# Inverse transform in front of P times V on TensorE, with ScalarE's two copies in that order

## What is computed

```python
# layer 0: window attention whose queries and keys are multiplied in the Fourier domain
qkv3 = ...                      # 1x1 convolution of the group-normalised x, 8x8 windows, 6 heads of 32
o = jnp.fft.irfft2(jnp.fft.rfft2(qp) * jnp.fft.rfft2(kp), s=(8, 8))    # per head and channel
attn = jnp.einsum('bhnd,bhmd->bhnm', o, vv) + bias[None]
attn = jax.nn.softmax(attn, axis=-1)
y = jnp.einsum('bhnm,bhmd->bhnd', attn, vv)
x = x + einsum('bchw,oc->bohw', y, proj_w) + proj_b
# layer 1: a Laplacian and a 1x1 convolution, of the group-normalised x
x = x + conv1x1(xn + laplacian(xn), merge_w) + merge_b
```

## Time and profile before

| | us |
|---|---|
| median of 3 runs | 6069.41 (6067.23 to 6069.91) |
| the profiled execution | 6063.48 |
| its span, first to last instruction | 6061.7 |
| TensorE busy (PE) | 5826.5 |
| VectorE busy (DVE) | 5059.8 |
| ScalarE busy (ACT) | 3165.5 |
| GpSimd busy (POOL) | 2011.1 |

### The profile page before, as it was taken

One profiled execution on the slowest core, in us unless ns is written; L12 is line 12 of the kernel. 1 busy time (PEld: TensorE's weight loads), 2 busy tenths in 40 slices (PEclk: granted clock), 3 DMA queues, 4 the chain that ended last, 5 costly groups with the idle time before them and its releaser, 6 DMA issues.

```text
span 6061.7 us, 210224 instructions
## 1 busy us (share of the span) xinstructions
PE 5826.5 (96%) x93708; PEld 5135.1 (85%) x93708; DVE 5059.8 (83%) x8287; ACT 3165.5 (52%) x6020; POOL 2011.1 (33%) x1286
## 2 busy tenths in 40 slices
PE   7999999999999999999999999999999999999987
PEld 5888888888888888888888888888888888888876
DVE  4777788888888888888888888888888888888876
ACT  2555555555555555555555555555555555555531
POOL 1333333333333333333333333333333333333310
PEclk9999999999999999999999999999999999999999
DMA  4221123323333233332333323332333322222235
GB/s 130 71 58 58 54 75 104 98 81 93 95 104 101 75 92 99 101 97 80 95 101 100 93 80 93 106 101 86 86 96 98 106 84 69 82 79 75 80 93 163
DMA packets 392599, 550.79 MB, mean 91 GB/s; under 512 B 24918, under 2 KB 284825, under 8 KB 391706
## 3 DMA queue, kind: packets, MB, share of 16 engines
q1 hardware_dynamic: 391708, 537.35, 30.9%
HBM read 335.93 MB, written 201.33 MB: 89 GB/s over the span
## 4 chain that ended last, share of the span: by engine, by line
PE 82%; DVE 8%; ACT 7%; issue 1%; DMA 1%; SPq 0%; DVEq 0%
PE b_q L481 22%; PE b_t L570 10%; PE b_s L587 7%; PE b_q L556 7%; PE b_t L546 6%; PE b_s L489 5%; PE b_s L486 5%; PE b_t L528 4%; PE b_s L432 3%; PE b_s L434 3%; PE b_t L518 3%; ACT qkh L940 2%; DVE qkl L874 2%; PE b_s L441 2%; PE b_s L443 2%; PE b_s L442 2%
## 5 line engine op out<-in xcount | busy, mean ns | idle before, releaser
L1047 POOL TENSOR_TENSOR probs<-probs,srec 128x768 f32<-128x768 f32 x512 | 880.7, 1720 | 2211.8 <-DVE srec L923 2211.8
L1036 POOL TENSOR_TENSOR probs<-probs,smax 128x768 f32<-128x768 f32 x512 | 754.1, 1473 | 1519.7 <-DVE smax L885 1519.7
L880 DVE TENSOR_TENSOR probs<-b_s,posb 128x768 f32<-128x768 f32 x512 | 488.3, 954 | 660.3 <-PE b_s L587 659.4
L940 ACT ACTIVATE vs<-b_q 128x192 f32<-128x192 f32 x1024 | 339.2, 331 | 1294.3 <-PE b_q L481 1294.3
L481 PE MATMUL b_q<-wnh,xh 128*128 128x288 f32 x2048 | 700.7, 342 | 67.0 <-DVE qkl L874 65.7
L874 DVE TENSOR_TENSOR qkl<-b_q,qkh 128x384 fp32r<-128x384 f32 x1024 | 566.5, 553 | 176.9 <-ACT qkh L940 139.7
L489 PEld LDWEIGHTS b_s<-yT,wp 128*128 128x128 f32 x4096 | 618.5, 191 | 52.3
L489 PE MATMUL b_s<-yT,wp 128*128 128x128 f32 x4096 | 622.4, 275 | 0.0
L486 PE MATMUL b_s<-yT,wp 128*128 128x256 f32 x2048 | 613.5, 381 | 1.5 <-DVE probs L880 0.9
L481 PE MATMUL b_q<-wnl,xhl 128*128 128x288 f32 x2048 | 606.5, 296 | 0.0
L481 PE MATMUL b_q<-wnh,xhb 128*128 128x288 f32 x2048 | 606.3, 296 | 0.0
(11 more groups left out here) (155 smaller groups left out, 13688.6 us busy)
## 6 DMA issues: line engine op xcount, KB each, us to landing
ld<-in_x SPq DMA_DIRECT2D x192, 512.0 KB, 4.6
late<-x_dram SPq DMA_DIRECT2D x112, 640.0 KB, 4.8
xs<-in_x SPq DMA_DIRECT2D x128, 512.0 KB, 5.4
x_dram<-late SPq DMA_DIRECT2D x128, 512.0 KB, 3.0
out<-late SPq DMA_DIRECT2D x128, 512.0 KB, 3.0
late<-x_dram SPq DMA_DIRECT2D x240, 192.0 KB, 5.4
xs<-in_x SPq DMA_DIRECT2D x128, 256.0 KB, 5.9
x_dram<-late SPq DMA_DIRECT2D x128, 256.0 KB, 3.7
```

The lines of the kernel that those rows point to most:

```text
L880: V.tensor_tensor(scored(i).rearrange("p (t q) m -> p t q m", q=4), scores.rearrange("p (t q m) -> p t q m", q=4, m=N), posb[:, :, :].unsq ...
L940: return A.activation(o, i, ACT.Copy)
L1036: P.tensor_tensor(probs[:, i % 2, :, :], probs[:, i % 2, :, :], smax[:, i % 2, :].unsqueeze(2).broadcast_to([128, 12, N]), ALU.subtract).t ...
L1047: P.tensor_tensor(probs[:, i % 2, :, :], probs[:, i % 2, :, :], srec[:, i % 2, :].unsqueeze(2).broadcast_to([128, 12, N]), ALU.mult).then_ ...
```

## The change

In TensorE's program o moves ahead of y; in ScalarE's program the copy of o (`osb`) moves ahead of the copy of y (`yT`). Nothing else differs, and no wait is added or dropped. After the change the matmuls of o stand on L542 and those of y on L556.

```diff
                 m_slot(2 * j + 1, pair)
+                if pair(1):
+                    pe.wait_ge(prod_done, pair(1)[1])
+                    if pair(0):
+                        pe.wait_ge(lo_out, 2 * j + 2)
+                    for k in range(6):
+                        for g in range(2):
+                            last = mm(o_out_ps[g * N:(g + 1) * N, k * N:(k + 1) * N],
...
+                    last.then_inc(o_mm, 1)
                 if pair(3):
                     k, n = pair(3)
                     pe.wait_ge(pT_out, n)
...
                     last.then_inc(y_mm, 1)
-                if pair(1):
...
-                    last.then_inc(o_mm, 1)
                 if pair(0):
                     pe.wait_ge(lo_out, 2 * j + 2)
...
+                if pair(1):
+                    act.wait_ge(o_mm, pair(1)[1])
+                    copy(osb[:, :, :].rearrange("p k n -> p (k n)"), o_out_ps).then_inc(o_out, 1)
                 if pair(3):
                     act.wait_ge(y_mm, pair(3)[1])
                     copy(yT[:, :, :, :].rearrange("p i w n -> p w i n"),
                          q_banks[:, 2:4, 0:3 * N].rearrange("p w (i n) -> p w i n", n=N)).then_inc(yT_out, 1)
-                if pair(1):
-                    act.wait_ge(o_mm, pair(1)[1])
-                    copy(osb[:, :, :].rearrange("p k n -> p (k n)"), o_out_ps).then_inc(o_out, 1)
```

More of the change, by code:

```diff
@@ L535, in _ @@
                 m_slot(2 * j + 1, pair)
+                if pair(1):
[5 more added lines that the diff above has]
+                            last = mm(o_out_ps[g * N:(g + 1) * N, k * N:(k + 1) * N],
+                                      prod[:, g * 6 + k, :, :].rearrange("p h d -> p (h d)"), inv[:, :],
+                                      start=True, stop=True)
+                    last.then_inc(o_mm, 1)
                 if pair(3):
```

## The result

| | before | after |
|---|---|---|
| median of 4 runs, us | 6068.32 (6065.76 to 6069.91) | 6115.02 (6109.53 to 6121.13) |
| the profiled execution | 6063.48 | 6117.48 |
| its span | 6061.7 | 6115.6 |

The change makes the kernel slower: the ratio is 1.0077, interval 1.0065 to 1.0089, which is 46.7 us (39 to 54). Forecast were +40 and 6109.4. The two profiled executions lie 54.0 us apart, 7 more than the medians, so a sum over their turns comes out some 7 us too large for the median.

A forecast was written before the change was run, and what follows sets the result against it. The prediction took TensorE, 82% of the chain, as the bound; 43.0 us for turns 76 to 511, plus 2 for earlier turns, less 4.8 at changes of image, gave +40, so 6109.4 us, range 6080 to 6132.

The forecast's parts named there:

- Part 1: In TensorE's stretch of o and y: exchanging their matmuls costs 0, bounded at 0.01 us a turn.
- Part 2: At t's second half: it waits for yT, 0.05 us late plus 0.08 for unhidden loads, 0.13 us a turn.
- Rival 1: At t's second half: loads are pulled ahead of the wait, only 0.05 is lost; +11 us, 6080; chance 0.10.
- Part 3, kind 2: Turns 76 to 511 with j mod 4 = 2: each pays 0.13 us; 28.3 us together with j mod 4 = 0.
- Part 3, kind 3: Turns with j mod 4 = 3: 14.2 us; o's wait for qkl replaces y's for probsT within 0.01.
- Part 3, kind 0: Turns 76 to 511 with j mod 4 = 0: each pays 0.13 us; 28.3 us together with j mod 4 = 2.
- Part 3, kind 1: Turns with j mod 4 = 1: VectorE holds s, so 103 of 109 cost 0; 0.8 us for the other six.
- The changes of image, -4.8: Around changes of image: VectorE is the bound for 37 turns' worth, TensorE's delay costs nothing there; -4.8 us.
- Turns before 76: Turns 3 to 75: o's 0.12 earlier start nearly pays back the 0.13; +2 us including late qkl.
- Rival 2: At t's second half: it isn't late, so only o's earlier start is left; -16 us, 6053; chance 0.04.

The follow-up runs named there:

- e2: The kernel before with only ScalarE's order changed (osb, then yT), TensorE keeping y, o, t; 6279.64 us against 6069.37, ratio 1.0349.
- e3: The kernel before with the change only in turns with j mod 4 = 2 from turn 76 on; 6082.82 us, ratio 1.0019.
- e4: The kernel before with the change only in turns with j mod 4 = 3 from turn 76 on; 6078.71 us, ratio 1.0017.
- e12: The kernel before with VectorE's L758 moved ahead of the remainder xhl (L927) in odd turns; 6083.65 us, ratio 1.0025.
- e9: The kernel before with the change only around changes of image (j mod 64 from 4 to 11 and 52 to 55); 6084.42 us against 6068.56, ratio 1.0028.
- e7: The changed kernel with ScalarE's copy yT cut to 64 of its 384 columns, result incomplete; 6082.26 us, ratio 1.0022.
- e11: The change in all turns but those around a change of image, with copy yT cut to 64 of 384 columns; 6070.03 us, ratio 1.0004.
- e1: The kernel before with only TensorE's order changed (o ahead of y), ScalarE's order kept; 6124.73 us against 6069.37, ratio 1.0093.
- e5: The changed kernel with the first product of t's first half done twice; 6144.65 us, ratio 1.0129.
- e8: The kernel before with half of o ahead of y and half behind it on TensorE, ScalarE's order kept; 6132.35 us, ratio 1.0106.
- e6: The kernel before with the first product of t's first half done twice; 6128.92 us, ratio 1.0100.
- e10: The kernel before with the change in all turns but those around a change of image; 6106.17 us, ratio 1.0064.

## Why the prediction was right, and where it was off

- *Part 1, the swap costs nothing.* Right: 1.54 against 1.55.
- *Part 2, 0.05 late and 0.08 for the loads.* Right: the half at 0.65, the next step at 0.25, load and matmul together 0.05 to 0.06 behind yT's end; e2 shows the 0.08 at a lateness of 0.44, e3 the 0.13 alone. Rival 1 falls. The load queue stood idle until yT ended: the pull-ahead of LDWEIGHTS past matmuls in flight, which the Trainium skill states in "TensorE: Matmul & The Clock Gate", Part 2, did not happen past an unmet wait. In kind 1, at 0.68, more is lost; the cover takes it.
- *Part 3, kind 2.* Right: 0.127 to 0.130 a turn, 13.5 us in e3 for a forecast half of 28.3.
- *Part 3, kind 3.* Right in itself: one wait took the place of the other within 0.01, 13.9 us forecast and measured.
- *Part 3, kind 0: the step that failed.* "218 x 0.13" took kind 0 as bound by TensorE everywhere. In 54 of its turns the slot at the start waits for VectorE's L880, so the delay that kind 3 hands on is absorbed (e4: -3.8; e2: 0.09 of 0.52). These 54 gave 2.2 us instead of 7.0. The whole kind gave 6.8 instead of 14.2, since at the changes of image it gains 0.37 a time besides, which kind 1 pays back.
- *Part 3, kind 1.* The cover held: 0.00 and +0.01 in steady turns, and e12 confirms that L758 is the cover. Of its 10.4 us instead of 0.8, 8.9 lie at the changes of image, where it pays back 0.37 a time of what kind 0 had just gained from the wait for probsT, and where s stops.
- *The changes of image, -4.8: too cheap by some 12 us.* The sum took VectorE as the bound there, so that TensorE's delay would cost nothing; with the 0.13 that it had already counted for these turns they came to about +2 (54 x 0.13 + 0.8 - 0.9 - 4.8). They took +14.0 in the trace of after, +15.9 in e9, and 13.4 in e7 without any late half. Where VectorE holds s the delay is indeed hidden (o to s 3.60 in both), but kinds 2 and 3 still pay their 0.13, and behind the waits come the stops in s and stretches at the lower clock.
- *Turns before 76.* +2 was forecast, +6.0 measured: turns 68 and 69, the first change of image, have 4.4 of it. In the others the gain and the wait cancel but for 0.01 to 0.02, as forecast. e7 shows both sides: with the wait gone they gain 0.12 each.

So +40 was close to +46.7 mostly because the mechanism of the forecast is the larger part, 31 to 33 us of it, and partly by luck: 4.8 us too much in 54 turns of kind 0 offset part of some 12 too little at the changes of image and 4 too little before turn 76. (In the profiled executions the miss is 14 us, in the medians 7.) Rival 2 named what would be left without the wait; in e11 each early turn has that gain, and turns 68 and 69 take it back.

**What the stops are.** All six kernels with o in front at the changes of image have them in s (L587 or its like, put down to issue: after 11.4 us, e1 13.0, e5 18.9, e7 17.6, e8 19.3, e9 6.7), and the longest of these, 0.9 to 2.3 us, come at the changes of image, most of them behind a wait for VectorE. The others have less of it: before 0.5, e2 none, e3 1.4, e4 5.2, e6 0.2, e10 2.8, e11 6.2, e12 0.7. But o in front isn't needed for every one: e10 and e11 leave turn 68 in the old order, and stop there inside t for 1.6 and 2.4 us, with the turns ahead of it changed; in e3, e4 and e6 that turn has at most 0.2 us more than in before. Instructions come by DMA: the page of after counts

```profile
q8 instruction: 750, 12.29, 0.8%
```

which is 16.4 KB a packet, and the Trainium skill, in "Runtime: NRT & Kernel Launch", Instruction fetch mechanics, has them refilled in 16 KiB blocks at a cost that is mostly hidden. The traces show that the stops are waits for such a block. TensorE's matmuls, weight loads and sequencer instructions are 192069 records, 256 for each packet; e5 and e6 have 2048 more, and 8 packets more. Number the records in program order. Every idle time of over 0.15 us in s or t that no wait explains, 173 of them in the 14 traces, ends at a matmul whose number leaves 192 or 193 when divided by 256: that is where a new packet's records begin. And it ends 1.2 to 1.8 us after the end of a packet on q8. For the stop in turn 117 of after, that packet ran from 1353.62 to 1354.68,

```profile
q8 instruction: 1, 0.02, 6.1%
```

(the DMA view of 1353.6 to 1354.7; packets, MB and share), and s went on at 1356.32. In before the packet of the same records had ended at 1345.40, 3.8 us ahead of the matmul that needs it. In after 18 packets start when TensorE has less than 100 records left before the first of theirs, in before 2.

**What stays open.** Why those packets start late: what sets the start of a packet was not tried. Nor do the runs separate the stops from the lower clock behind them: the stops at the changes are 5.9 us of after, and in the stretches at the lower clock the matmuls take nearly twice as long. That these two are what makes e9's 15.9 us is argued from where they lie, not shown by a run that takes them away.

## To carry to other kernels

When two producers on one engine change places, look at what stood between each of them and the consumer of its copy: the filler that was between y and the half that overwrites its bank was o, and a wait that is missed by 0.05 us cost 0.13 here, since the weight loads wait too. Check for each kind of turn whether a delay is paid, absorbed by a wait further on, or hidden, up to the start of the next turn; and look apart at the rare stretches, because a group that waits in them can expose more than its wait. A stop in the middle of a group that no semaphore explains may be a wait for instructions: see whether it always falls on the same place when the engine's instructions are counted by 256, and look for the packet of the instruction queue in front of it. An engine whose order is changed for one consumer may meet another engine's work in memory, as xhl did.

## What the runs showed of the hardware

- A wait that is ended by ScalarE lets TensorE start 0.05 to 0.06 after the copy's recorded end (yT, probsT); VectorE's L874 in front of o and L927 in front of L481 take 0.15, and L880 in front of L432 0.10 to 0.11. o and L481 have more than one semaphore to wait for; whether that makes the difference wasn't tried.
- One more change of the shape of weights costs 0.14 us (e8: 1.69 against 1.55); loads of t's weights that nothing hides cost 0.08 (0.25 to the next step against 0.17).
- TensorE's instructions come in packets of 256 records, 16 KiB each. In all 14 traces the first matmul of a packet's records runs 1.19 us or more after the packet's end, and no packet starts more than 299 records ahead of its first; a packet that comes late stops TensorE in the middle of a group, for up to 2.4 us.
- After stops and waits of TensorE around a change of image the granted clock fell to its lower level in the middle of the kernel, for 3.4 to 6.8 us at a time; two matmuls of L481 were then 0.24 apart instead of 0.13.
- A VectorE TENSOR_TENSOR on SBUF and GpSimd's hold each other up: whichever starts second is longer by 0.50 (GpSimd's, 1.97 against 1.47, 254 times in before) or by 1.05 us (VectorE's, 1.74 against 0.69, 109 times in e12).
